# A two-layer graph attention kernel: the pairs of scratch memsets between the table gathers are taken out

## The reference

```python
h = relu(layernorm(x))
scores = where(adj > 0, h @ w0 @ inp.T, NEG_PAD)          # layer 0
x = x + softmax(scores / 0.07, axis=1) @ inp
h = relu(layernorm(x)) @ W                                # layer 1
e = leaky_relu((h @ a_src)[:, None] + (h @ a_dst)[None, :], 0.2)
valid = (adj > 0) & (h.sum(axis=1) != 0)[None, :]
att = softmax(where(valid, e, NEG), axis=1)               # 0 where not valid
att = where(att >= 1e-4, att, 0) * valid.sum(axis=1)[:, None]
out = x + elu(h + att @ h)
```

## Time and profile before

| | |
|---|---|
| median of 3 runs | 720.17 us (720.14 to 721.64) |
| span of the profiled execution, first to last instruction | 713.4 us |
| own time of that execution beside its span | not printed on the page |
| busy: DVE, ACT, PE, POOL | 506.1, 407.4, 393.6, 370.8 us |
| memsets of the pause | 72, 533 ns each, 38.4 us |
| gathers from the tables | 144, 985 to 1085 ns on average |
| DMA | 262 GB/s on average, above 310 up to some 445 us, then 42 to 204 |

### The profile page before, as it was taken

The page is one execution under the profiler, slowest core; times in us unless marked ns, Lnnn a source line. Parts: engine busy times, 40 slices in busy tenths (PEclk is TensorE's granted clock), DMA queues, the critical chain, the costliest instruction groups (busy, mean ns, idle before and its releaser), DMA issues.

```text
span 713.4 us, 9730 instructions
## 1 busy us (share of the span) xinstructions
PE 393.6 (55%) x2916; PEld 270.0 (38%) x2947; DVE 506.1 (71%) x2125; ACT 407.4 (57%) x424; POOL 370.8 (52%) x425
## 2 busy tenths in 40 slices
PE   3244465576767575859576756754702601526653
PEld 1011133253535362626253534453601500516653
DVE  0009778898989897979798989898307313559985
ACT  6348496777989888797988988622201100022222
POOL 5000060606161525243377877788787887888800
PEclk9557697978979888888999999875655555657788
DMA  8999989999898999898999999511111221114322
GB/s 326 412 425 419 367 312 418 333 374 364 295 413 318 412 343 410 331 398 338 389 366 386 399 404 400 204 56 43 53 44 46 57 87 46 42 54 120 110 67 92
DMA packets 37480, 186.79 MB, mean 262 GB/s; under 512 B 7856, under 2 KB 8112, under 8 KB 18864
## 3 DMA queue, kind: packets, MB, share of 16 engines
q1 hardware_dynamic: 28208, 167.02, 60.2%
q0 software_dynamic: 9216, 19.11, 9.1%
HBM read 179.73 MB, written 6.37 MB: 261 GB/s over the span
## 4 chain that ended last, share of the span: by engine, by line
DVE 44%; POOL 25%; issue 12%; PE 7%; DMA 5%; ACT 5%; DVEq 0%; SPq 0%; POOLq 0%
POOL arena L823 14%; DMA arena<-in_adj 5%; PE K L1433 5%; POOL mean_w L818 4%; DVE keys L1033 3%; DVE G L1144 3%; ACT R_all L906 2%; DVE RTp L1203 2%; ACT arena L877 2%; POOL E L823 2%; POOL X L794 2%; DVE cand L1063 2%; DVE mi_w L1184 2%; POOL arena L794 1%; DVE cand L1051 1%
## 5 line engine op out<-in xcount | busy, mean ns | idle before, releaser
L877 ACT ACTIVATE arena<-arena,half_c 128x2048 fp8e4<-128x2048 int32 x144 | 281.2, 1997 | 35.8 <-DMA arena<-in_adj 28.1
L794 POOL DMA_INDIRECT X<-in_L_gnn_input,idx_all x132 | 131.3, 994 | 255.1 <-DVE idx_near L1115 217.2
L1433 PE MATMUL K<-arena,bits 128*128 128x512 fp8e4 x576 | 167.6, 431 | 50.0 <-ACT arena L877 24.8
L823 POOL DMA_INDIRECT arena<-table,idx_near x96 | 104.2, 1085 | 28.5 <-issue 22.3
L1433 PEld LDWEIGHTS K<-arena,bits 128*128 128x128 bf16 x576 | 59.2, 108 | 93.4 <-ACT arena L877 30.1
L1033 DVE MAX8 keys<-K 128x8 int32<-128x128 f32 x192 | 42.4, 281 | 55.4 <-PE K L1433 55.3
L823 POOL DMA_INDIRECT E<-table,idx_near x48 | 47.3, 985 | 14.4 <-issue 12.2
L1445 PE MATMUL G<-g,R_all 128*128 128x128 bf16 x324 | 28.2, 243 | 39.0 <-DVE G L1144 24.8
L1445 PEld LDWEIGHTS G<-g,R_all 128*128 128x128 fp8e4 x324 | 23.3, 110 | 48.8 <-issue 28.2
L906 ACT CAST R_all<-G 128x512 fp8e4<-128x512 f32 x36 | 19.8, 587 | 34.4 <-PE G L1467 20.6
L818 POOL MEMSET mean_w<- 128x512 f32 x72 | 38.4, 533 | 2.1
(11 more groups left out here) (249 smaller groups left out, 1016.2 us busy)
## 6 DMA issues: line engine op xcount, KB each, us to landing
arena<-in_adj SPq DMA_DIRECT2D x144, 1024.0 KB
table<-hs SPq DMA_DIRECT2D x12, 262.0 KB, 8.3
hs<-table SPq DMA_DIRECT2D x12, 262.0 KB, 2.7
E<-in_L_gnn_input SPq DMA_DIRECT2D x1, 3072.0 KB, 25.8
out_x<-x_all SPq DMA_DIRECT2D x12, 256.0 KB
x_all<-in_x SPq DMA_DIRECT2D x1, 2560.0 KB, 19.5
X<-in_L_gnn_input,idx_all POOLq DMA_INDIRECT x132, 5.7
arena<-table,idx_near POOLq DMA_INDIRECT x96, 2.5
```

The lines of the kernel that those rows point to most:

```text
L794: pool.indirect_dma_start(out=x_of(b)[:, e, :], out_offset=None, in_=inp, in_offset=bass.IndirectOffsetOnAxis(ap=idx_all[:, at:at + 1], ax ...
L823: pool.indirect_dma_start(out=E[g][:, t, :], out_offset=None, in_=tables[g], in_offset=bass.IndirectOffsetOnAxis(ap=idx_near[:, t, g:g + 1 ...
L877: nc.scalar.activation(sign[:, load % RING, :], ring[:, load % RING, :], ACT.Sign, bias=half_c[:], scale=1.0, saturate=False).then_inc(sig ...
L1433: last = mm(bank_[:], bits[:, third * TB + j, :], sign[:, load % RING, j * FOLD:(j + 1) * FOLD], start=False, stop=(third == G - 1 and j = ...
```

## The change

The helper `pause`, the two linked memsets, is removed, and with it its call behind each fourth gather of `records`; the constant that set the distance goes too. All gathers, waits and their order stay.

```diff
-    FEW = 4
...
-                def pause():
-
-                    for _ in range(2):
-                        link(pool.memset(mean_w[:], 0.0))
-
                 def records(g, first, last):
 
                     for t in range(first, last):
...
                         ).then_inc(E_r[g][t // Q], 16)
-                        if t % FEW == FEW - 1:
-                            pause()
```

## The result

The changed kernel takes 694.42 us, the median of four executions (690.20 to 695.36). The four of the kernel before shown with them lie at 714.82 to 721.64; the ratio is 0.966 (95%: 0.961 to 0.972). A second measurement of the same two kernels gave 695.85 (695.48 to 698.95) against 714.68 (712.50 to 718.01), ratio 0.974 (0.969 to 0.979). So the change saves 19 to 26 us.

What follows compares the result with a forecast made beforehand. POOL's program order was taken to set the time from 459 us on. Of 28.3 us for 26 pairs, the caps at the store and DVE left 21.3: 720.2 - 21.3 = 698.9 us, range 695.0 to 703.0.

Steps and rivals of the forecast that it cites:

- the price per pair of 1.09: Between two POOL gathers: a pair of memsets stretches the pitch from 1.25 to 2.34 us, so each costs 1.09.
- Both caps: Waiting for the last table store loses 2.6 to 2.9 us; DVE's work in the last three steps loses some 4.4.
- The base: Starting time of the sum, 720.2 us, from which the gain of 21.3 was taken.
- Collisions: POOL gathers beside long DVE operations: 0 to 1.54 us each, before as after; no net change, 3 us either way.
- that term: Six pairs on POOL's path ahead of block 11's `X` rows, 6 x 1.09 us gained there.
- the operation at 482.26: DVE operation beside a pair, costing POOL nothing; without the pair, the next gather would be held from 483.4 to 484.0.
- Block 11's own chain: From block 11's first `X` product, near 531, to the last table store's landing at 569.5; moves earlier as a whole.
- DVE's step: DVE's own work per take of 8 tiles, 15.06 us, bounding the last three steps once the pairs go.
- rival C: Gathers in every slot slow DVE's one-input operations in the last steps and block 11's chain: 702.5 us; chance 0.15.
- B: No cap holds at the store or in DVE's steps; all 28.3 and 0.5 come through: 691.4 us; chance 0.05.
- D: The gather queue backs up in the last run of 56 gathers, each waiting 2.5 us: 751 us; chance 0.04.
- E: Pairs only fill a wait: gathers are limited to their mean pitch of 1.52 us, nothing gained, 720; chance 0.03.

Runs made afterwards that it cites:

- The four sets: Changed kernel with pairs put back: 9 in the stream (no difference seen), 6 ahead of block 11's rows (stage +6.8), 7 behind them (+4.3), 8 in the last steps (+1.6).

## Why the prediction was right, and where its sizes were off

*The mechanism held.* POOL set the time behind the stream, and the price per pair of 1.09 came back at full where nothing hid it (6.8 for six). The pairs in the stream cost nothing that the times can show. Both caps are there, each shown by a set that cost less than its pairs: seven behind block 11's rows 4.3, eight in the last steps 1.6. POOL's wait at the store was 3.25 and 3.8 us where 2.6 was forecast, and DVE waits for no gather in the last three steps, as forecast. The four sets add up to 12.7 of the stage's 23.0; the six pairs behind tiles 0 to 15 of the third table and 40 to 47 of the second were not put back alone (6.5 by their price). The 3.8 that are left are not accounted for: no two sets were put back together.

*The base was wrong by 5 us, the largest miss.* I kept the 6.8 between span (713.4) and median (720.17) as time around the span. In the later executions, where both are known, the time is 1.5 to 2.0 above the span (714.68 and 713.1; 695.36 and 693.6). The profiled execution thus took about 715.1 and was one of the shorter ones; 713.4 + 1.7 - 21.3 = 693.8 would have been the sum. In the profiles the spread lies in the stream: the first `X` gather of block 7, ahead of every pair, came at 349.06 before and at 352.18 after. Why it drifts is open.

*That the forecast came so near is in part luck.* Against the profiled execution of the changed kernel (695.36) the base was 5.1 too high and the gain in the stage 2.8 too low, which together would have given 691.0; but in that execution the stage began 4.3 us later than forecast (463.61 against 459.81 - 0.5), of which 3.1 were there at block 7, ahead of every pair.

*Collisions, taken at no change, gained.* On the way to block 11's rows three gathers took 2.10, 1.53 and 2.36 before, and 1.44, 0.94 and 2.19 after: 1.4 us of the 1.6 by which that term exceeds its 6.5. And that step was mistaken in one example: the operation at 482.26 is not of the kind that holds a gather; it reads PSUM, and with or without a pair behind it nothing is held. The Trainium skill, SBUF — State Buffer, "Who interferes with whom", makes the distinction by SBUF inputs; the runs bear it out (0.94 beside a PSUM input, 1.2 to 2.5 with two from SBUF). That a writer is not held, the trace of before shows at another place, POOL and DVE in order of time:

```profile
610.67 1.12 POOL L818 MEMSET mean_w<- 128x512 f32 x2
```

```profile
611.14 1.76 DVE L1377 TENSOR_TENSOR RTp<-RT_all,above 128x1536 f32<-128x1536 fp8e4 x1
```

The pair ran into a multiplication with both inputs in SBUF and took its usual 1.12.

*Block 11's own chain*, from its first product to the landing of the store, was taken as 38.5 and took 37.1 and 37.6. In the first of the two PE had a higher share of its clock, as the rows for that stretch show (the third number from the end is PE's granted clock, before and after):

```profile
538.10:574.30 36.20, 16.37 (x97) 14.84 (x97) 19.68 (x101) 6.29 (x14) 29.27 (x35) 0.55 0.20 52
```

```profile
533.80:568.60 34.80, 15.42 (x97) 13.89 (x97) 19.24 (x101) 6.29 (x14) 26.51 (x27) 0.60 0.26 61
```

0.55 against 0.60, means of stretches in which both levels occur; in the second profile it was 0.55 again, so this explains one of the two at most.

*DVE's step* was taken as 15.06 and took 14.6 to 14.9: three steps 44.2 and not 45.2. The copy and the scalar operation that a gather held before for 0.46 and 0.44 took 0.17 and 0.22 (once 0.28) in the last steps; rival C, slower DVE operations, went the other way. The part behind the last take was 35.0 and 35.1 instead of 34.4.

*The other rivals.* B fell: DVE does not wait for gathers at the end, and POOL does at the store. D and E fell: the 56 gathers behind 571.53 keep the pitch of 1.25 but for those beside a DVE operation.

## What to carry to other kernels

Before a stage that one engine sets is shortened, look for the slack of every other input at each point where the stage meets it: here 28.3 us of removed work met 4.8 us at a store and 0.1 us a step at DVE, and 23 came through. Compare kernels by stages counted from a common event, and fix the base of a sum by span against span, not by a median of other executions. Here a gather that POOL issued was held by a DVE multiplication with both inputs in SBUF; moving the small one of them to PSUM left the multiplication at 1.75 and gave 6.5 us where POOL was the bound, 1.5 at most where DVE was.

## What the runs showed of the hardware that I had not expected

In the ten profiles in which all these multiplications read SBUF alone, a gather that started inside one ended 0.81 to 0.83 us behind it (176 of 178; the other two 0.85 and 0.86), wherever inside it started; so its cost is set by where it starts, from 0.25 to 1.54 us. The 149 gathers that were under way when one began took 0.94 to 0.96: they were not held. The same multiplication of 128 x 1536 takes 1.75 or 1.76 us with its second input in SBUF or in PSUM.
